# Values' products in runs of four key blocks, with nine buffers, in a two-layer attention kernel

## What is computed

```python
# layer 0: 8 heads of 32 channels
h = group_norm(x) * gn_w + gn_b
q, k, v = split(qkv_w @ h + qkv_b)             # per head: 32 x 1024
w = softmax(q.T @ k / sqrt(32))                # 1024 x 1024 per head
x = x + proj_w @ (v @ w.T) + proj_b
# layer 1: one head, q and k of 32 channels, v of 256
out = (Wv @ x) @ softmax((Wq @ x).T @ (Wk @ x)).T
y = gamma * out + x
```

## Time and profile before

| | |
|---|---|
| median of three runs | 1522.86 us (1522.31 to 1525.66) |
| the profiled execution | 1526.38 us, its span 1524.6 us |
| TensorE busy | 1483.1 us |
| GpSimd busy | 1185.9 us |
| VectorE busy | 1099.2 us |
| ScalarE busy | 746.4 us |
| mean granted clock | 0.977 |

### The profile page before, as it was taken

How to read it: one execution, slowest core, us unless ns; L and a number is a source line. 1 busy time by engine, 2 the same in 40 slices (tenths; PEclk the granted TensorE clock), 3 DMA queues, 4 the chain that set the end, 5 groups by cost and what they waited for, 6 DMA issues and landing times.

```text
span 1524.6 us, 20547 instructions
## 1 busy us (share of the span) xinstructions
PE 1483.1 (97%) x7216; PEld 891.4 (58%) x7216; DVE 1099.2 (72%) x1922; ACT 746.4 (49%) x1373; POOL 1185.9 (78%) x548
## 2 busy tenths in 40 slices
PE   8899999999999999999999999999999999999878
PEld 6444445577455855558555775558555684457447
DVE  4777878777787778877687777877788686765343
ACT  2256455544565354653555445653546435554411
POOL 2189988985989679995989859896799959898703
PEclk9699899999999999999999999999999999999979
DMA  5233031301403014120413014030231214000100
GB/s 140 55 96 68 17 87 46 83 10 49 112 22 84 15 56 102 39 65 28 112 50 79 12 51 111 22 84 15 60 100 41 60 31 109 22 1 8 49 21 28
DMA packets 47143, 85.24 MB, mean 56 GB/s; under 512 B 11072, under 2 KB 21184, under 8 KB 47040
## 3 DMA queue, kind: packets, MB, share of 16 engines
q1 hardware_dynamic: 46896, 83.74, 21.7%
q10 hardware_dynamic: 144, 0.20, 0.1%
HBM read 18.29 MB, written 8.39 MB: 17 GB/s over the span
## 4 chain that ended last, share of the span: by engine, by line
PE 87%; DVE 5%; SPq 3%; issue 2%; ACT 1%; DMA 1%; POOL 0%; ACTq 0%; DVEq 0%; POOLq 0%
PE work L635 15%; PE st L551 15%; PE pv L582 15%; PE pv L560 14%; PE work L698 7%; PE work L669 4%; DVE mpart L931 3%; PE work L705 3%; PE work L657 3%; SPq L386 3%; PE st L543 2%; PE work L643 2%; PE rec L599 2%; PE work L663 1%; PE rec L612 1%
## 5 line engine op out<-in xcount | busy, mean ns | idle before, releaser
L902 POOL TENSOR_TENSOR acc<-acc,probs 128x1024 f32<-128x1024 f32 x380 | 889.7, 2382 | 49.1 <-ACT probs L773 49.1
L773 ACT ACTIVATE probs<-st 128x512 f32<-128x512 f32 x1152 | 611.2, 601 | 446.1 <-PE st L551 326.7
L931 DVE TENSOR_REDUCE mpart<-work 128x1 f32<-128x512 f32 x1008 | 635.8, 680 | 164.8 <-PE work L635 163.2
L635 PE MATMUL work<-ks,qs 96*128 96x512 f32 x1008 | 427.0, 464 | 8.7 <-DMA ks<-part_hi 3.6
L551 PE MATMUL st<-qs,ks 98*128 98x512 f32 x1024 | 398.3, 436 | 6.2 <-DMA qs<-mrow 3.1
L902 POOL TENSOR_TENSOR acc<-probs 128x1024 f32<-128x1024 f32 x64 | 150.9, 2376 | 165.6 <-ACT probs L773 165.3
L635 PEld LDWEIGHTS work<-ks,qs 96*128 96x128 f32 x1008 | 191.7, 193 | 148.9 <-DVE mpart L931 87.9
L551 PEld LDWEIGHTS st<-qs,ks 98*128 98x128 f32 x1024 | 193.7, 191 | 126.1 <-ACT probs L773 67.8
L560 PE MATMUL pv<-probs,vt 128*32 128x512 f32 x2048 | 247.9, 602 | 0.0
L582 PE MATMUL pv<-probs,l_vt 128*128 128x256 f32 x1024 | 240.2, 383 | 0.5 <-ACT raw L839 0.5
L582 PEld LDWEIGHTS pv<-probs,l_vt 128*128 128x128 f32 x1024 | 193.2, 191 | 34.1 <-ACT probs L773 5.9
(11 more groups left out here) (82 smaller groups left out, 940.0 us busy)
## 6 DMA issues: line engine op xcount, KB each, us to landing
qs<-part_hi SPq DMA_DIRECT2D x120, 128.0 KB, 2.4
ks<-part_hi SPq DMA_DIRECT2D x120, 128.0 KB, 2.4
xa<-in_x SPq DMA_DIRECT2D x16, 512.0 KB, 4.3
y<-in_x SPq DMA_DIRECT2D x8, 1024.0 KB, 5.6
out<-raw SPq DMA_DIRECT2D x32, 256.0 KB, 2.2
qs<-part_lo SPq DMA_DIRECT2D x60, 128.0 KB, 2.4
ks<-part_lo SPq DMA_DIRECT2D x60, 128.0 KB, 2.4
l_qs<-part_hi SPq DMA_DIRECT2D x32, 64.0 KB, 2.0
```

The source lines that it names most:

```text
L635: last = mm(bank, qs[g][0:HI_HI_LO, c, j, tb * P:(tb + 1) * P], ks[g][0:HI_HI_LO, j, half * HALF:(half + 1) * HALF], start=True, stop=True)
L773: nc.scalar.activation(probs[:, n % PRING, half * HALF:(half + 1) * HALF], st[:, (2 * n + half) % ST_BANKS, :], ACT.Exp).then_inc(s_exp1 i ...
L902: pool.tensor_tensor(a, first, probs[:, n % PRING, :], ALU.add).then_inc(s_add0, 1)
L931: last = dve.reduce_max(mpart[:, 4 * j + tb, half:half + 1], bank, AX.X)
```

## The change

- TensorE issues the values' products for four key blocks together, at n % 8 == 1.
- `probs` has nine buffers instead of six. Space for them comes from `raw1`, which now lies in `xa` (in the first batch the part it served for QF lies in `y`), and from `mrow`, which has one pair for both groups. The loads of `xa` wait for the outputs of the batch before; the first load of `y` stands later in SyncE's order.
- In the first batch GpSimd leaves out the last key block of each chunk, and the sum's matmul takes it from `probs`, as the epilogue did with two.
- ScalarE runs the entries of the first two stops of a slot with n % 8 == 1 before the exponential.
- The four tables are new. Of them, STEADY's sums, layer 1 and norm entries and the epilogue's stand here (three stops make a slot); the rest is left out.

```diff
-PRING = 6
+PRING = 9
...
 STEADY = {
-    "sums": (13, 14, 14, 18, 29, 59, 72, 74, 89, 97, 120, 124, 133, 147, 148, 153, 153, 154, 157, 157),
-    "layer1": (20, 35, 35, 35, 49, 70, 104, 113, 134),
-    "norm": (32, 35, 35, 41, 49, 63, 64, 97, 100, 109, 109),
+    "sums": (10, 14, 14, 16, 23, 72, 74, 75, 100, 118, 134, 135, 135, 141, 146, 153, 154, 154, 154, 157),
+    "layer1": (4, 7, 32, 33, 38, 55, 88, 112, 139),
+    "norm": (27, 34, 35, 42, 52, 70, 84, 100, 109, 110, 120),
...
 EPILOGUE = {
-    "sums": (2, 3, 3, 3, 3),
-    "layer1": (0, 0, 5, 6, 7, 9, 9, 10, 12, 13),
-    "maxima1": (11, 11, 11, 11, 15, 15, 15, 15, 15, 15, 15, 15, 15, 15, 15, 15, 16, 17),
+    "sums": (3, 3, 6, 6, 10),
+    "layer1": (0, 0, 0, 0, 10, 10, 18, 26, 27, 50),
+    "maxima1": (26, 35, 35, 35, 41, 41, 41, 41, 45, 45, 45, 46, 46, 46, 46, 46, 46, 46),
...
-        raw1 = sb("raw1", [P, 4, KT, QUARTER])
...
-        mrow = [[sb(f"mrow{g}{c}", [16, 2, P], F32R) for c in range(2)] for g in range(GROUPS)]
+        mrow = [sb(f"mrow0{c}", [16, 2, P], F32R) for c in range(2)]
...
+        def adds_until(b, ci):
+            return ADDS0 * b + 14 * ci - 2 * min(4 * b + ci, 4)
...
         def wait_added(eng, i, b):
             ci, blk, pair = i // 16, i % 16 // 2, i % 2
-            eng.wait_ge(s_add0, ADDS0 * b + 14 * ci + 2 * (max(blk, 1) - 1) + pair + 1)
+            if b == 0 and blk == SB - 1:
+                wait_summed(eng, ("SUM", ci // 2, ci % 2), "steady" if ci == 3 else "first", ci // 3)
+            else:
+                eng.wait_ge(s_add0, adds_until(b, ci) + 2 * (max(blk, 1) - 1) + pair + 1)
...
+        def raw1(c):
+            return xa[:, c // 2, c % 2 * HALF:(c % 2 + 1) * HALF].rearrange("p (m t) -> p m t", m=KT)
...
                 if kind in ("first", "steady"):
                     sp.wait_ge(s_h, KT * (b + 1))
+                    if b > 0:
+                        for c in range(4):
+                            sp.wait_ge(s_out[c], 16 * b)
                     for k in range(KT):
                         sp.dma_start(xa[:, k, :], x_v[b + 1, :, k, :]).then_inc(s_x, 16)
-                if kind == "first":
-                    sp.dma_start(y[:, :, :], x_v[0]).then_inc(s_y, 16)
...
                 if kind != "epilogue":
                     max_rows(1, 0, kind, b)
+                if kind == "first":
+                    sp.wait_ge(s_stack[1], 16 * STACK_DMAS)
+                    sp.dma_start(y[:, :, :], x_v[0]).then_inc(s_y, 16)
...
+                    left = LEFT if kind == "epilogue" else 1 if bb == 0 else 0
...
+                    for blk in range(left):
+                        for j in range(GH):
+                            last = mm(rec[CH * j:CH * (j + 1), :], ones[:, 0:CH],
+                                      probs[:, (last_slot(ci) - 2 * left + 1 + 2 * blk + j // 2) % PRING,
+                                            (j % 2) * HALF:(j % 2 + 1) * HALF],
+                                      start=False, stop=blk == left - 1, tile_position=(0, CH * j))
...
                     if n == 1 and kind not in ("prologue", "first"):
-                        product_l0(SLOTS - 3, b - 1)
-                        product_l0(SLOTS - 1, b - 1)
-                    elif n % 4 == 1 and n - 5 in units and unit_use(n - 2)[0] == 0:
+                        for m in range(SLOTS - 7, SLOTS, 2):
+                            product_l0(m, b - 1)
+                    elif n % 8 == 1 and n - 9 in units and unit_use(n - 2)[0] == 0:
...
-                        product_l0(n - 4, b)
-                        product_l0(n - 2, b)
+                        for m in range(n - 8, n, 2):
+                            product_l0(m, b)
...
+                    stops = [plans[kind][STOPS * n + k] for k in range(STOPS)]
+                    before = stops[0] + stops[1] if n % 8 == 1 else []
+                    for e in before:
+                        use_entry(e, kind, b)
                     if n in units:
                         exponentials(n, kind, b)
...
-                    if blk == 0 or (i >= L0_UNITS - 2 * LEFT and b == B - 1):
+                    if blk == 0 or (blk == SB - 1 and b == 0) or (i >= L0_UNITS - 2 * LEFT and b == B - 1):
                         continue
...
                     if what == "T":
...
+                        if g:
+                            dve.wait_ge(s_mrow[0][c], 32 * (b + 1))
+                        elif n > 0:
+                            dve.wait_ge(s_mrow[1][c], 32 * n)
```

More of the change, by code:

```diff
@@ L63 @@
     "qf": (7, 7, 8, 8),
[L64 to L70, removed]
[6 rows of a table removed]
+    "maxima0": (12, 12, 16, 21, 22, 22, 24, 24, 24, 24, 24, 26, 26, 28, 28, 28),
+    "qk1": (158, 193, 208, 208),
+    "norm": (29, 29, 29, 42, 48, 64, 64, 107, 108, 110, 112),
+    "sums": (63, 72, 95, 97, 108, 112, 122, 151, 155, 157, 162, 166, 185, 203, 206),
+    "v0": (193, 211),
+    "v1": (32, 50),
+    "maxima": places(4, 1, 0, 1, 1, 0, 0, 0, 0, 0, 0, 0, 0, 0, 0, 4, 0, 1, 0, 0, 0, 1, 0, 0, 2, 0, 0, 1, 0, 0, 1,
[6 rows of a table added]
 }
 LAST = {
[L79 to L84, removed]
[6 rows of a table removed]
+    "maxima1": (58, 60, 62, 63, 66, 73, 81, 82, 83, 88, 91, 94, 95, 95, 110, 112, 125, 125),
+    "sums": (9, 11, 26, 30, 32, 56, 57, 67, 111, 122, 143, 152, 155, 155, 156, 163, 165, 166, 167, 167),
+    "sums1": (159, 160, 163, 169, 170, 170, 171, 174, 174, 174, 175, 175),
+    "layer1": (14, 24, 38, 39, 41, 67, 70, 106, 113),
+    "v1": (32, 119),
+    "maxima": places(0, 0, 2, 0, 2, 0, 0, 1, 0, 0, 3, 1, 1, 0, 1, 0, 0, 1, 0, 1, 2, 0, 2, 0, 0, 0, 0, 0, 3, 0, 1,
[6 rows of a table added]
 }
 EPILOGUE = {
-    "sums": (2, 3, 3, 3, 3),
[3 rows of a table removed]
+    "sums": (3, 3, 6, 6, 10),
[3 rows of a table added]
 }
@@ L436, in max_rows @@
                     dst = qs[g][r:r + 1, c, :, :].bitcast(F32).rearrange("o j (t x) -> o (j t) x", x=P)
-                    sp.dma_start(dst, mrow[g][c][:, part, :].bitcast(F32)).then_inc(s_mrow[g][c], 16)
+                    sp.dma_start(dst, mrow[c][:, part, :].bitcast(F32)).then_inc(s_mrow[g][c], 16)
             def step(kind, b):
@@ L595, in fill_rec @@
                     _, g, c = e
-                    n_acc = chunk_no(e, b) + 1
-                    pe.wait_ge(s_add0, 14 * n_acc - (2 * LEFT if kind == "epilogue" else 0))
+                    ci = 2 * g + c
+                    bb = b - 1 if ci == 3 else b
+                    left = LEFT if kind == "epilogue" else 1 if bb == 0 else 0
+                    pe.wait_ge(s_add0, adds_until(bb, ci + 1) - (2 * LEFT if kind == "epilogue" else 0))
                     for j in range(GH):
@@ L600, in fill_rec @@
                                   acc[:, c, j // 2, (j % 2) * HALF:(j % 2 + 1) * HALF], start=True,
-                                  stop=kind != "epilogue", tile_position=(0, CH * j))
-                    if kind == "epilogue":
-                        pe.wait_ge(s_exp0, 2 * L0_UNITS * B)
-                        for blk in range(LEFT):
-                            for j in range(GH):
-                                last = mm(rec[CH * j:CH * (j + 1), :], ones[:, 0:CH],
-                                          probs[:, (SLOTS - 2 * LEFT + 2 * blk + j // 2) % PRING,
-                                                (j % 2) * HALF:(j % 2 + 1) * HALF],
-                                          start=False, stop=blk == LEFT - 1, tile_position=(0, CH * j))
+                                  stop=not left, tile_position=(0, CH * j))
+                    if left:
+                        wait_exp(pe, last_slot(ci), bb)
+                    for blk in range(left):
[4 more added lines that the diff above has]
+                                      start=False, stop=blk == left - 1, tile_position=(0, CH * j))
                 else:
@@ L754, in exponentials @@
                     act.wait_ge(s_pv0, 32 * B)
-                    act.wait_ge(s_add0, ADDS0 * B - 2 * LEFT)
+                    act.wait_ge(s_add0, adds_until(B, 0) - 2 * LEFT)
                     wait_summed(act, ("SUM", 1, 1), kind, b)
@@ L815, in use_bank, with use_entry @@
                 last.then_inc(s_wa, 1)
+            def use_entry(e, kind, b):
+                if e[0] in SCALAR_USES or e[0] in ("QK", "QF", "QK1"):
+                    use_bank(e, kind, b)
+                elif e[0] == "H":
+                    act.wait_ge(s_stats, 6 * (b + 2))
+                    wait_used(act, ("G2",), kind, b)
+                    if e[1] == 0 and kind != "prologue":
+                        act.wait_ge(s_w, w_base(kind, b) + place[kind][("VT", 1, 1)] + 1)
+                    nc.scalar.activation(h[:, e[1], :], xa[:, e[1], :], ACT.Identity, bias=aff_b[:, e[1]:e[1] + 1],
+                                         scale=aff_a[:, e[1]:e[1] + 1]).then_inc(s_h, 1)
             def step(kind, b):
@@ L819, in step @@
                 for n in range(SLOTS):
-                    entries = [e for k in range(STOPS) for e in plans[kind][STOPS * n + k]]
```

(24 more changed lines are left out.)

24 lines of the change are left out of this document (12 added, 12 removed), and 38 rows, old and new, of tables (EPILOGUE, FIRST, LAST, STEADY).

## The result

The kernel after takes 1512.78 us (median of 4 runs, 1511.23 to 1515.13), the kernel before in the same session 1523.33 us (4 runs, 1522.31 to 1525.66). The ratio is 0.9929, 95% interval 0.9916 to 0.9942: 10.5 us faster, where 25.3 were forecast. The profiled execution took 1515.13 us, its span is 1513.1 us. The time lies in the predicted range and the sign is right, but the forecast gain is more than twice the measured one.

What follows compares the result with a forecast made beforehand. TensorE's queue was taken to bound the six middle batches; gains of 15 (middle), 4.4 (first batch), 2.4 (last batch) and 3.5 us (epilogue) sum to 25.3, giving 1497.6 us from the 1522.9 median, range 1482 to 1517.

Steps and rivals of the forecast that it cites:

- Entries into the narrow shape: TensorE's switches into 128x32 tiles: seven fewer per batch, 2.8 us each batch, 16.8 us over six middle batches.
- my 0.40: TensorE's assumed cost in us of entering and leaving the 128x32 shape once, taken from readings of 0.33 to 0.44.
- What longer runs cost: Middle batches: waits for work banks as VectorE idles during runs of four; 0.3 us a batch taken.
- ScalarE's wait for the first product: At n%8 = 1 the exponential waits for the run's first product; claimed hidden by the other three products (2.6 us).
- First batch: First batch: GpSimd's dropped additions let the order avoid the low-clock stretch; 5 us gained, net 4.4 us.
- the 7.5 us at a low clock: First batch, 163 to 178 us: time counted as lost because TensorE's matmuls ran at 0.66 mean clock.
- Nine buffers, shared space, y's load: Buffers gain nothing in middle batches; shared space and moved loads cost nothing, at most 2 us a batch.
- Last batch and epilogue: Six runs saved before slot 58 give 2.4 us; the epilogue's reordered values and QK1 give 3.5 us.
- The slower rival: Every run of four is followed by one reduction's wait, 2.6 us lost per batch: 1544 us; chance 0.12, all slower cases.

Runs made afterwards that it cites:

- singles_old_order: The kernel before with every values' product in a run of its own, one every second slot instead of two every fourth; 1561.43 us, ratio 1.0236.
- half_both pair: The kernels before and after, each with row maxima and exponentials working on half of each bank; 1492.99 us (before) and 1470.54 us (after).
- after_again: The kernel after, unchanged, measured again beside other variants on one chip; 1513.71 us, ratio 0.9924 to the kernel before.
- all_additions: The kernel after with GpSimd's additions of all blocks kept in the first batch too; 1509.75 us, ratio 0.9901 to the kernel before.
- first_batch_as_before: The kernel after with the first batch's old table, products in pairs and all GpSimd additions put back; 1511.41 us, ratio 0.9907 to the kernel before.
- ring9_pairs_old_order: The kernel before with only the nine buffers and shared space added, keeping old tables, pairs and all additions; 1527.16 us, ratio 1.0013.
- fours_old_order: The kernel before with nine buffers, shared space and products in runs of four, on the old tables; 1582.22 us, ratio 1.0376.
- before_half_both: The kernel before with row maxima and exponentials working on half of each bank; 1492.99 us, ratio 0.9773 to the kernel before.

## Why the prediction missed

- **Entries into the narrow shape: right.** 2.8 us a batch predicted; 2.7 to 3.0 by the count and the price of singles_old_order. Two small errors cancel in it: eight entries fewer for seven, at 0.34 to 0.39 us for 0.40. On the rule that TensorE drains at a change of tiling mode (the Trainium skill, TensorEngine Tiling (Array Packing), Key Properties): the runs agree that something is paid at each change, at most 0.37 to 0.39 us for both ways. They don't decide between my 0.40 and the 0.33 us that the prediction estimated from the Trainium skill, since a part can be stalls.
- **What longer runs cost: this step failed.** I had bounded it between nothing and 0.68 us per run and taken 0.3 us a batch, "because VectorE has three times the slack". Measured are 1.4 to 2 us a batch (2.7 to 3.0 saved, 1.0 to 1.3 left), some 0.2 us per run. The mechanism named there, VectorE idle in the run and denser behind it, is seen. Wrong was its measure. 41 us of free time in a batch say little where three banks are all that can be stored: as I read it, an engine's slack is only of use at the moment when it has a full bank before it. And ScalarE's wait for the first product I had called hidden, while ScalarE is as much a releaser. The half_both pair shows that the two account for most of it: 1.0 us a batch gained with both as they are (1.3 in after_again), 0.7 to 1.4 with fast maxima, 1.9 to 2.4 with fast maxima and fast exponentials. 6 x (2.5 - 1.0) = 9 us of the miss.
- **First batch: failed.** 4.4 us predicted, nothing measured. The step took the 7.5 us at a low clock to be the price of waiting for GpSimd. GpSimd is not what bounds this batch: all_additions and first_batch_as_before lose nothing by giving it its work back. VectorE's maxima are a good part of it: faster ones take 8.3 us off before and 5.8 after. Faster exponentials beside them take off 1.4 us more before and 3.9 more after, so ScalarE has a part too. The time that the better clock gave back at 163 to 178 us was lost elsewhere in the batch; that the clusters of maxima are the place is not shown.
- **Nine buffers, shared space, y's load: nearly right.** Put at nothing; ring9_pairs_old_order is 0.5 to 3.5 us slower by its interval, which may be up to a quarter of the miss.
- **Last batch and epilogue: right in sum** (5.4 us for 5.9), with luck in the parts. Ahead of the final sum 2.4 us were to be gained and none was (167.5 us for 166.1); behind it 3.5 us were forecast and 6.8 came, a part of which is the 3.7 us of QK1 and values moved ahead. That GpSimd still sets the final sum was wrong: its last addition is done 2.6 us before.
- **The slower rival** asked for 0.35 us per run. fours_old_order is beyond that (stalls up some 9 us a batch, over 1.1 us per run), the kernel after below it. What decides between the two is not the run's length but the order. The rival was real, and only the new tables keep it away.

What is open: how the 1.4 to 2 us split over particular chains within a batch, what the two odd batches of before_half_both wait for, and whether a still better order for runs of four exists; none of it was tried.

## What to carry to other kernels

Taking work out of the bounding engine's queue in many small pieces pays their price; gathering the remaining work in longer runs takes away the pauses in which the engines behind it caught up, and the three banks here store only some 2 us for them (3 x 0.68). So cost a longer run against the stored work of every engine that empties or fills a bank, not against its free time in the stage. And read such a change together with its order: with the run length crossed against the old and the new order, the runs of four range here from 7.4 us a batch lost to 1.0 gained.

## What the runs showed of the hardware

- A change into and out of 128x32 tiles costs TensorE 0.34 to 0.39 us in the middle of a full queue: 15 more of them a batch, 5.5 to 5.9 us. It is paid per run and not per product: a run of 8 instructions takes 1.00 us to the next start, one of 16 takes 1.85, one of 32 takes 3.57.
- A better clock in one stretch of the first batch was no gain: 0.89 between 163 and 178 us in the kernel after, 0.66 in first_batch_as_before, and the batch takes 157.6 and 157.7 us. TensorE was at the low level (0.5, 1.2 GHz) for a part of that stretch in each.
- In the epilogue the clock did show: the same code took 42.2 us at a mean granted clock of 0.90 and 40.3 at 1.00.
